# Scan stage of an attention and state-space block: fewer half-states summed by transfers, wide weights loaded in pieces, slot tables laid out anew

## The reference, cut to what matters

```python
xr, z = jnp.split(xm @ W_in, 2, axis=-1)                 # 512 -> 2 x 1024
u = silu(causal_conv(xr, W_conv) + b_conv)
dt, Bm, Cm = jnp.split(u @ W_x, [64, 80], axis=-1)       # N = 16 states
delta = softplus(dt @ W_dt + b_dt)
h = exp(delta * A) * h + (delta * u) * B_t               # for each time, channel and state
y = sum over the 16 states of h * C_t
ssm_out = ((y + u * D_param) * silu(z)) @ W_out
attn_out = heads @ Wproj + bproj
full = silu(ln(concat[ssm_out, attn_out]) @ W_full + b_full)
out = x + gate * full
```

## Time and profile before

| what | value |
|---|---|
| median of 3 runs | 3813.27 us (3806.51 to 3813.51) |
| profiled execution, its own time | 3809.16 us |
| its span, first to last instruction | 3807.3 us |
| mean granted TensorE clock | 0.939 |
| PE busy | 86% |
| DVE busy | 67% |
| ACT busy | 52% |
| POOL busy | 50% |

### The profile page before, as it was taken

The page is one execution under the profiler, slowest core; times in us unless marked ns, Lnnn a source line. Parts: engine busy times, 40 slices in busy tenths (PEclk is TensorE's granted clock), DMA queues, the critical chain, the costliest instruction groups (busy, mean ns, idle before and its releaser), DMA issues.

```text
span 3807.3 us, 36220 instructions
## 1 busy us (share of the span) xinstructions
PE 3292.6 (86%) x12362; PEld 1708.2 (45%) x12362; DVE 2557.9 (67%) x3208; ACT 1963.5 (52%) x3386; POOL 1899.3 (50%) x1163
## 2 busy tenths in 40 slices
PE   7899999999999997777988887888888888888867
PEld 3344444444444443444544544544444544444543
DVE  3253535344444434787897897997997997987974
ACT  2234433343434333655765764764765774775642
POOL 0122221212121212767676776786786776776672
PEclk9999999999999999789999998998998999999978
DMA  5101010110101021214334333423433332333231
GB/s 179 69 1 47 1 47 1 47 43 5 48 1 47 1 78 32 63 52 114 86 105 111 100 101 101 130 75 102 128 85 114 107 111 89 105 114 94 67 100 45
DMA packets 117880, 280.37 MB, mean 74 GB/s; under 512 B 11889, under 2 KB 12001, under 8 KB 114626
## 3 DMA queue, kind: packets, MB, share of 16 engines
q1 hardware_dynamic: 101314, 226.73, 17.6%
q0 software_dynamic: 13824, 50.34, 7.0%
q10 hardware_dynamic: 2560, 0.98, 0.1%
HBM read 193.85 MB, written 33.83 MB: 60 GB/s over the span
## 4 chain that ended last, share of the span: by engine, by line
PE 21%; DVE 14%; issue 8%; DMA 6%; POOL 5%; ACT 5%; SPq 0%; POOLq 0%; DVEq 0%; ACTq 0%
PE bank L1563 9%; DVE HS L1437 6%; DVE acc L1446 5%; PE bank L1578 5%; POOL HS L1174 4%; PE bank L1649 3%; PE bank L1664 2%; DMA acc<-terms 2%; DMA brep<-b_d 2%; DMA comb<-ot_d 2%; DVE U L1471 2%; ACT bank L1266 1%; PE bank L1647 1%; POOL DU L1189 1%; PE bank L1587 1%
## 5 line engine op out<-in xcount | busy, mean ns | idle before, releaser
L1174 POOL TENSOR_TENSOR HS<-DU,brep 128x1024 f32<-128x1024 f32 x512 | 1229.4, 2413 | 508.3 <-PE bank L1578 445.0
L1437 DVE TENSOR_TENSOR_SCAN HS<-bank,HS 128x1024 f32<-128x1024 f32 x512 | 1164.0, 2280 | 190.4 <-ACT bank L1266 168.6
L1578 PE MATMUL bank<-ident,HS 128*128 128x128 f32 x4096 | 628.4, 298 | 310.7 <-DVE acc L1446 238.7
L354 POOL TENSOR_TENSOR PR<-PR,rrec 128x512 f32<-128x512 f32 x256 | 260.0, 1039 | 1160.5 <-DVE rrec L612 1160.5
L1266 ACT ACTIVATE bank<-delta,aneg 128x511 f32<-128x511 f32 x1024 | 660.2, 683 | 280.3 <-DVE HS L1437 279.5
L1578 PEld LDWEIGHTS bank<-ident,HS 128*128 128x128 f32 x4096 | 503.1, 152 | 595.1 <-DVE HS L1437 297.1
L1446 DVE SCALAR_TENSOR_TENSOR acc<-bank,C,acc 128x512 f32<-128x512 f32 x768 | 534.1, 736 | 97.5 <-PE bank L1578 61.9
L1563 PE MATMUL bank<-XM,w_l 128*128 128x512 f32 x1024 | 494.0, 627 | 29.0 <-DVE U L1471 15.0
L441 ACT ACTIVATE PR<-bank,nsmax 128x512 f32<-128x512 f32 x256 | 173.4, 682 | 373.2 <-DVE nsmax L608 373.2
L714 PE MATMUL bank<-w_l,NT 128*128 128x512 f32 x768 | 344.7, 597 | 4.9 <-ACT NT L393 4.9
L1563 PEld LDWEIGHTS bank<-XM,w_l 128*128 128x128 f32 x1024 | 193.5, 200 | 240.3 <-issue 200.3
(11 more groups left out here) (173 smaller groups left out, 3893.1 us busy)
## 6 DMA issues: line engine op xcount, KB each, us to landing
brep<-b_d SPq DMA_DIRECT2D x256, 256.0 KB, 3.4
acc<-terms POOLq DMA_DIRECT2D x96, 512.0 KB, 5.2
w_l<-in_L_cond_W_in SPq DMA_DIRECT2D x14, 2048.0 KB, 9.0
w_l<-in_L_cond_W_full SPq DMA_DIRECT2D x8, 2048.0 KB, 10.3
w_l<-in_L_cond_W_out SPq DMA_DIRECT2D x7, 2048.0 KB, 11.0
X<-in_x SPq DMA_DIRECT2D x8, 1024.0 KB, 5.2
x_d<-X SPq DMA_DIRECT2D x8, 1024.0 KB, 4.7
xm_d<-XM SPq DMA_DIRECT2D x8, 1024.0 KB, 3.9
```

The lines of the kernel that those rows point to most:

```text
L354: nc.gpsimd.tensor_tensor(p, p, rrec[:, hp % 2, t, e:e + 1].to_broadcast([P, T]), ALU.mult).then_inc(pnorm, 1)
L1174: nc.gpsimd.tensor_tensor(HS[:, u % DEEP], DU[:, chunks(j, s), :], brep[:, m % 3, :].unsqueeze(1).to_broadcast([P, UC, T]), ALU.mult).then ...
L1437: nc.vector.tensor_tensor_scan(h, dA[:, u % 2].rearrange("p i t -> p (i t)"), h, 0.0, ALU.mult, ALU.add).then_inc(scanned, 1)
L1578: last = nc.tensor.transpose(y_bank[t % 2][:, i * P:(i + 1) * P], h, ident[:])
```

## The change

`SPARED` loses state 6 in both halves, so that a batch has four spared half-states of 32. `load_wide` loads a quarter of a weight, cut along its rows (512 KB of a 2 MB weight, 256 KB of Wproj), and SP issues the four quarters in four consecutive slots. PE waits for all four quarters of a weight, before the same product as before. The slot tables for half0 and half1 get new numbers; those of the last batch's tail and of the first batch's front that have names of their own stay. The amount of work of every other kind is unchanged. The diff, cut to its core:

```diff
+PIECES = 4
...
-        def load_wide(eng, name):
+        def load_wide(eng, name, j):
             src = {"xr": a["L1_cond_W_in"][:, 0:DI], ...}[name]
-            eng.dma_start(wide[name], src.rearrange("(c p) n -> p c n", p=P)).then_inc(arrived[name], 16)
+            n = src.shape[0] // P // PIECES
+            c = slice(j * n, (j + 1) * n)
+            eng.dma_start(wide[name][:, c, :], src.rearrange("(c p) n -> p c n", p=P)[:, c, :]).then_inc(arrived[name], 16)
...
-                load_wide(sp, "xr")
-                load_wide(sp, "z")
+                for name in ("xr", "z"):
+                    for j in range(PIECES):
+                        load_wide(sp, name, j)
...
-        SPARED = ((3, 6, 9), (4, 6, 9))
+        SPARED = ((3, 9), (4, 9))
...
-        PE_XR = ((0, 0), (1, 2), (2, 3), (3, 4), (5, 6), (6, 6), (6, 7), (8, 10))
-        PE_Z = ((10, 11), (11, 11), (15, 15), (21, 21), (22, 22), (22, 24), (24, 24), (26, 26))
-        PE_XD = (12, 12, 13, 14)
-        PE_DT1 = (15, 17, 19, 19)
-        PE_C = 18
-        PE_P = ((29, 29), (29, 30), (31, 31), (33, 33))
-        PE_DT0 = (3, 4, 8, 9)
-        PE_O = ((2, 2, 2, 3), (5, 5, 5, 7), (14, 15, 15, 15), (21, 21, 22, 22))
-        PE_CT = ((11, 11), (15, 16), (22, 23), (26, 26))
-        PE_F = ((12, 12, 12, 13), (17, 18, 19, 19), (23, 24, 25, 25), (27, 28, 29, 30))
+        PE_XR = ((0, 0), (1, 1), (2, 3), (4, 4), (5, 6), (7, 7), (7, 8), (9, 9))
+        PE_Z = ((10, 10), (11, 11), (15, 15), (21, 21), (22, 22), (23, 23), (24, 25), (26, 26))
+        PE_XD = (12, 13, 13, 14)
+        PE_DT1 = (16, 16, 19, 19)
+        PE_C = 17
+        PE_P = ((29, 29), (30, 30), (31, 31), (33, 33))
+        PE_DT0 = (3, 4, 9, 9)
+        PE_O = ((2, 2, 3, 3), (5, 5, 6, 7), (14, 14, 15, 15), (20, 20, 21, 22))
+        PE_CT = ((11, 11), (15, 15), (23, 23), (26, 27))
+        PE_F = ((12, 12, 12, 13), (17, 17, 17, 19), (23, 23, 25, 25), (27, 28, 28, 30))
...
-        ACT_SILU_U = {12: (0, 1, 2, 3), 13: (4, 5, 6, 7)}
+        ACT_SILU_U = {6: (0, 1, 2, 3), 12: (4, 5, 6, 7)}
...
-        ACT_DT0 = {5: (4, 5), 11: (6, 7)}
-        ACT_SILU_Z = {4: (0, 1, 2, 3), 22: (4, 5, 6, 7)}
-        ACT_P = {29: 0, 32: 1, 33: 2, 37: 3}
+        ACT_DT0 = {6: (4, 5), 9: (6, 7)}
+        ACT_SILU_Z = {3: (0, 1, 2, 3), 30: (4, 5, 6, 7)}
+        ACT_P = {30: 0, 31: 1, 33: 2, 34: 3}
...
-        DVE_XD, DVE_C = 15, 18
+        DVE_XD, DVE_C = 14, 18
...
-        POOL_DU0 = {5: 4, 11: 5, 17: 6, 21: 7}
-        POOL_SKIP, POOL_ADD0 = {2: 0, 3: 1, 4: 2, 5: 3, 8: 4, 10: 5, 13: 6, 15: 7}, {2: 0, 3: 1, 4: 2, 5: 3}
+        POOL_DU0 = {10: 4, 11: 5, 14: 6, 24: 7}
+        POOL_SKIP, POOL_ADD0 = {0: 0, 1: 1, 2: 2, 3: 3, 4: 4, 7: 5, 15: 6, 16: 7}, {0: 0, 8: 1, 9: 2, 10: 3}
...
-        SP_B, SP_OUT, SP_OT, SP_GATE, SP_XM, SP_PROJ, SP_FULL = 13, 13, 27, 21, 13, 25, 5
+        SP_B, SP_OUT, SP_OT, SP_GATE, SP_XM, SP_PROJ, SP_FULL = 19, 15, 22, 26, 6, 26, 9
...
-        SP_XR, SP_Z = 20, 5
+        SP_XR, SP_Z = 23, 2
...
-                def weights(name, *key):
-                    sp.wait_ge(ring.full, ring.at(*key))
-                    load_wide(sp, name)
+                def weights(name, j, *key):
+                    if j in range(PIECES):
+                        sp.wait_ge(ring.full, ring.at(*key))
+                        load_wide(sp, name, j)
...
-                    if s == of(p, SP_FULL, 0):
-                        weights("full", p, "p3")
+                    weights("full", s - of(p, SP_FULL, 0), p, "p3")
...
-                                pe.wait_ge(arrived["full"], (p + 1) * 16)
+                                pe.wait_ge(arrived["full"], (p + 1) * PIECES * 16)
```

More of the change, by code:

```diff
@@ new lines, in mix @@
+        PE_C = 17
[4 more added lines that the diff above has]
+        PE_F = ((12, 12, 12, 13), (17, 17, 17, 19), (23, 23, 25, 25), (27, 28, 28, 30))
+        ACT_CONV0 = {0: 0, 2: 1, 3: 2, 5: 3, 6: 4, 8: 5, 9: 6, 11: 7}
+        ACT_UD = {0: (0, 1), 1: (2, 3), 4: (4, 5), 7: (6, 7)}
+        ACT_SILU_U = {6: (0, 1, 2, 3), 12: (4, 5, 6, 7)}
@@ new lines, in mix @@
+        ACT_Z = {13: 0, 14: 1, 17: 2, 21: 3, 23: 4, 24: 5, 26: 6, 28: 7}
+        ACT_DT1 = {18: (0, 1), 20: (2, 3)}
+        ACT_DT0 = {6: (4, 5), 9: (6, 7)}
+        ACT_SILU_Z = {3: (0, 1, 2, 3), 30: (4, 5, 6, 7)}
+        ACT_P = {30: 0, 31: 1, 33: 2, 34: 3}
+        ACT_O = {5: 0, 9: 1, 17: 2, 23: 3}
+        ACT_LN = {8: 0, 11: 1, 19: 2, 25: 3}
+        ACT_NORM = {12: 0, 14: 1, 22: 2, 26: 3}
+        ACT_CT = {12: (0, 0), 13: (0, 1), 17: (1, 0), 18: (1, 1), 24: (2, 0), 25: (2, 1), 27: (3, 0), 28: (3, 1)}
@@ L971, in mix @@
+        ACT_OUT = {37: (0, 1, 2, 3)}
+        DVE_CONV = {1: 0, 2: 1, 4: 2, 5: 3, 6: 4, 8: 5, 9: 6, 10: 7}
+        DVE_XD, DVE_C = 14, 18
+        DVE_STATS = {6: 0, 8: 1, 16: 2, 23: 3}
+        DVE_NEWTON = {9: 0, 13: 1, 19: 2, 25: 3}
+        DVE_F = {14: 0, 20: 1, 26: 2, 32: 3}
+        POOL_DU1 = {19: 0, 20: 1, 23: 2, 28: 3}
+        POOL_DU0 = {10: 4, 11: 5, 14: 6, 24: 7}
+        POOL_SKIP, POOL_ADD0 = {0: 0, 1: 1, 2: 2, 3: 3, 4: 4, 7: 5, 15: 6, 16: 7}, {0: 0, 8: 1, 9: 2, 10: 3}
         POOL_ADD1 = {0: 4, 1: 5, 2: 6, 3: 7}
-        POOL_OUT = {35: 0, 37: 1, 38: 2, 40: 3}
@@ L1119, in half0 @@
                             tail(p, s)
-                            if b + 1 < B and s == SP_XR:
-                                weights("xr", p, "o3")
+                            if b + 1 < B:
+                                weights("xr", s - SP_XR, p, "o3")
                 def half1(b, n, p):
@@ L1128, in half1 @@
                             front(n, s)
-                            if s == SP_OUT:
-                                weights("out", n, "xr7")
-                            if p is not None and s == SP_Z:
-                                weights("z", p, "f3")
+                            weights("out", s - SP_OUT, n, "xr7")
+                            if p is not None:
+                                weights("z", s - SP_Z, p, "f3")
                         if p is not None:
@@ L1138, in half1 @@
                             load_heads(b)
-                        if s == (SP_PROJ if n is not None else SP_PROJ_END):
-                            weights("proj", *((n, "z7") if n is not None else (p, "f3")))
+                        weights("proj", s - (SP_PROJ if n is not None else SP_PROJ_END), *((n, "z7") if n is not None else (p, "f3")))
                 load_xm(0)
@@ L1593, in gates @@
                             if c == 0:
-                                pe.wait_ge(arrived["z"], max(n, 1) * 16)
+                                pe.wait_ge(arrived["z"], max(n, 1) * PIECES * 16)
                             ring.wait_free(pe, n, f"z{c}")
@@ L1605, in front @@
                                 pe.wait_ge(xm_in, (n + 1) * 16)
-                                pe.wait_ge(arrived["xr"], max(n, 1) * 16)
+                                pe.wait_ge(arrived["xr"], max(n, 1) * PIECES * 16)
                             ring.wait_free(pe, n, f"xr{c}")
@@ L1644, in attention @@
                                 pe.wait_ge(ot_in, (b + 1) * 16)
-                                pe.wait_ge(arrived["proj"], (b + 1) * 16)
+                                pe.wait_ge(arrived["proj"], (b + 1) * PIECES * 16)
                             ring.wait_free(pe, b, f"p{t}")
@@ L1658, in tail @@
                             if t == 0:
-                                pe.wait_ge(arrived["out"], min(p + 1, B - 1) * 16)
+                                pe.wait_ge(arrived["out"], min(p + 1, B - 1) * PIECES * 16)
                             ring.wait_free(pe, p, f"o{t}")
```

16 lines of the change are left out of this document (2 added, 14 removed).

## The result

The changed kernel takes 3756.6 us (median of 4 runs, 3753.7 to 3759.5), against 3811.4 for the kernel before in the same comparison: a ratio of 0.9856 (95% interval 0.984 to 0.9871), 1.4% faster. The forecast was 3768, 1.2% faster, in a range of 3715 to 3820.

A forecast was written before the change was run, and what follows sets the result against it. DVE was taken to bound the stage, with waits filling the other 37 us of a 276.6 us period. Terms summed to -6.6 us a period, -46 over seven, -43 in all, giving 3768 us, range 3715 to 3820.

The forecast's parts named there:

- (a): State 6 on DVE: eight adds cost 5.5 us a period, 2.8 each half; ACT and POOL relief counts for nothing alone.
- (b): Silu of u in slots 6 and 12, half1: the 4.22 us ACT wait goes; with state 6's adds -1.4 us a period.
- (c): Late row of B and late sum, half1: POOL's row wait and state 6's transfer wait go, -2.8 us a period.
- (d): Products for z, slots 20 to 26: at most two half-products a slot shorten PE's longest wait of 3.4, -2.4 us a period.
- (e): Projection, slots 29 to 31: the 8.79 us wait goes, three overruns of 2.0 come back, -2.8 us a period.
- (g): Half0 slots 10 to 13: state 6's adds 2.8 us plus W_full's last piece 1.0 late, +3.8 us a period.
- (f): Start of half0, slot 2: two W_out half-products instead of three, -1.0 us; silu of z moved one slot costs nothing.
- Rival A: Nearly all waits go: DVE's idle time falls from 37 to 18 us a period, 3720 us; chance 0.14.
- B: The waits move: DVE waits for PE instead of ACT, adds paid in both halves, 3807 to 3821 us; chance 0.10.
- C: W_full stands late at PE's slot 12 of half0, lateness paid each period, 3834 us; chance 0.16 for all slower ways.
- D: The change does not do what it says: state 6 is still transferred somewhere; no chance worth a number.

The follow-up runs named there:

- x3: The changed kernel with each wide weight loaded whole in one transfer (PIECES = 1) instead of four pieces: 3735.6 us, ratio 0.9803 to the kernel before.
- x1: The changed kernel with state 6 spared again in both halves, all else as changed: 3811.2 us, ratio 0.9999 to the kernel before.
- x2: The kernel before, on its old tables, with state 6 added by DVE and nothing else: 3779.3 us, ratio 0.992.
- x6: The changed kernel with both silu groups of u back in slots 12 and 13: 3807.1 us, ratio 0.9985 to the kernel before.
- x10: The whole-weights variant (x3) with the store of B and the load of W_out back in SP's slot 13: 3742.7 us, ratio 0.9822 to the kernel before.
- x9: The changed kernel with the old slots for the z products and for ACT's fetches of them: 3759.5 us, ratio 0.9871 to the kernel before.
- x5: The changed kernel with the old projection layout (products, ACT's fetches, SP's slots for heads and Wproj): 3786.3 us, ratio 0.9932 to the kernel before.
- x4: The kernel before with wide weights in four pieces and nothing else, old tables, state 6 spared: 3789.0 us, ratio 0.9948.
- x7: The changed kernel with W_full's pieces two SP slots later, 11 to 14 instead of 9 to 12: 3809.8 us, ratio 0.9993 to the kernel before.

## Why the prediction was right, and where its terms were not

The time and both halves came out near the sum, and the mechanism it named, waits of DVE behind ACT, PE and transfers, is where the gain came from. That the halves agree to within half a microsecond is luck: terms of the wrong size, and one of the wrong sign, made up for each other. In half0 the forecast +2.8 and the measured +2.4 have different contents, adds and a late weight in the one, mostly the pieces (x3) in the other. The terms, each against the run that undoes it:

| term | forecast a period | measured | by |
|---|---|---|---|
| (a) state 6 on DVE | +5.5, half of it hidden | -6.3 in half1, 0 in half0 | x1 |
| the same on the old tables | | -4.0 and +0.7 | x2 |
| (b) silu in slots 6 and 12 | -4.2 without the adds | -6.6 | x6 |
| (c) late row | -1.4 | -1.1 | x10 (whole weights) |
| (d) products for z | -2.4 | -0.3 | x9 |
| (e) projection | -2.8 | -4.0 | x5 |
| (g) adds beside the W_full product | +2.8 | 0 | x1 |
| (f) start of half0 | -1.0 | about 0 | the trace, no run |
| (g) last piece of W_full late | +1.0 | 0.3 in one period of seven | the trace |
| all weights in pieces | 0 | +2.0 in half0, +1.2 in half1 | x3 |

- **(a) has the wrong sign in half1.** The step that failed is "ACT's and POOL's gain counts for nothing alone, since both idle". ACT idled on the mean, and in slots 13 and 14 it did not. I had read the earlier trace rows as waits for an accumulating transfer of 4.7 us and gave only 1.4 of it to state 6. x1 shows 3.76 us for its landing and 5.11 through the queue of ACT.
- **(b) is right in its cause and undersized.** I asked only who waited for the decay and not who waited for the fetch of the z product behind the same group.
- **(c) is right in size and half right in its way.** The late row costs 1.1 us (x10), but not through a wait of DVE for POOL. And "the longer (3.3) is state 9's and stays" failed: it went too. In the kernel before that wait is 1.1 to 3.3 us, 2.0 on average; with only state 6 added (x2) all of DVE's waits for transfers in half1 are 0.6 on average, and in the changed kernel 0.1.
- **(d) failed.** The step that failed took DVE's longest wait for PE as the overrun of a slot with three half-products, and priced it by the run of 7.36 us. x9 has the same slots, the run takes 5.32, and 0.65 of the wait is left; so it is in five of seven periods of the kernel before. I had priced the term from one of the two periods where it is longer. In both of these DVE had stood 3.3 us for state 9's transfer just before; in the other five 1.1 to 1.8. But x2 and x4 each have a run of 7.0 us without so long a wait, so why the clock was low there stays open.
- **(e) was too small, and two of its signs did not come.** The new layout leaves DVE waits of 4.0, 1.9 and 2.0 us at the projection, where three overruns of 2.0 were forecast; the wait that it removes would have been 11.8 with the rest of the new slots, not 8.8 (x5). ACT's wait for the first product is 9.18 us, not under 5, and the clock of the stretch 0.83, not near 1.0: the first product's eight records took 5.88 us, the next eight 3.70. The gain does not need either. ACT now forms its decay first and waits afterwards, so that DVE is not held.
- **(f) gained nothing.** In each of the seven half0s DVE's wait for PE fell from 2.42 to 0.64 us, and a wait of 1.78 for ACT came right behind it. In ACT's queue the silu of z, moved one slot ahead, stands in front of that decay; the step that failed is "I cost at nothing". The two kernels are level again at the next scan. After:

```profile
2366.20 2.29 DVE L1440 TENSOR_TENSOR_SCAN HS<-bank,HS 128x1024 f32<-128x1024 f32 x1 [1.78 <-ACT bank L1269]
```

- **(g)** PE waited for W_full in one period of seven, by 0.3 us. The estimated arrival, 0.3 to 2.5 us late, was at the edge of right. The pieces' price came another way: a later landing of the transfer beside them, and a lower clock in the product (x3). That a load in slot 9 costs more than one in slot 5 was not tested with whole weights.
- **Two counts were wrong.** The forecast 112 adds a period are 104, eight more than the 96 before, as (a) itself says; and the store of B is five slots behind the copy of x_dbl (19 and 14), not four. Neither entered the sum.

The parts do not add up: (b), (e) and state 6 undone alone are 17 us a period, and the change gave 6.9. With state 6 spared again, and also with the silu groups moved back, DVE waits for PE at the same place of half1 (5.11 us in x1, 4.85 in x6), behind a z product's fetch that is late in ACT's queue. So these two at least are not independent. Why the change as a whole gained what it did is therefore shown for each part against the changed kernel, not as a sum.

Rival A did not come: DVE's idle time fell to 25 us a period, not to 18. Of the others, B is the nearest to x1: with state 6 still spared the waits do move and the time is that of before. C is priced by x7: the mechanism costs every microsecond, and pieces two slots or some 8 us later wait 7.0 us, so the changed kernel stands within about 1 us of it. (It names "the same queues"; the trace has the rows and the pieces on SP's queue and the accumulating transfers on POOL's.) D did not arise.

On the Trainium skill, "DMA: Bandwidth & Descriptors", section "Bandwidth": its rule to batch transfers to 1 MiB or more spoke against the pieces. x3 agrees with its direction, 21 us for the whole weights; x4, on the old tables, does not: 0.5% faster with the pieces. Its reason (a smaller share of peak bandwidth) was not tested by itself. The estimate of 3.2 us for 512 KB, by the fit in "Anatomy of one DMA", which is stated for transfers that GpSimd issues, is far below the trace, where W_full's pieces, issued by SP, took 6.7 us in the median of a period, beside rows of B and accumulating transfers.

## What to carry to other kernels

Where work is moved off the fullest engine by a scaling and a transfer, price the place and not the unit: to spare one state (2.8 us of adds) cost 8.9 us of waits in half1, gained nothing in half0, and the four spared half-states that stayed saved together what their adds would have cost. Mean idle time of the engine that takes over says nothing about the slots in question; look at what stands behind the new instruction in its queue, and who needs that. When two edits come together (here pieces and slots), undo each alone before keeping both. And before a wait is priced, look for it in every period: one of 3.4 us stood in two periods of seven, and in the others it was 0.65.

## What the runs showed of the hardware that was not expected

A 512 KB piece of a wide weight takes longer to land than I had interpolated (4.5 us): over the seven periods of the changed kernel 5.7 us in the median for W_in and 6.4 for W_full, against 5.6 for 1 MB in one transfer. The transfers that POOL issues land later with them: a median of 5.9 us in a half0 beside pieces, 4.9 beside one whole weight, and 6.0 against 5.0 over the seven periods.
